# Scores and contexts of two graphs in one stretch of TensorE, in every second slot

## The chip, the cores and the metric

The kernel runs on one core of a Trainium2 chip. The metric is the device time of one launch in microseconds (us).

## The reference

Two layers of masked attention over 128 graphs of 128 nodes with 384 features, 6 heads of 64, each behind a layer norm with relu, with a residual sum. The adjacency matrix of a graph is the mask. Everything is float32.

```python
h = jnp.maximum(_layernorm(x, axis=-1), 0.0)
q = _heads(h @ Wq + bq)
k = _heads(h @ Wk + bk)
v = _heads(h @ Wv + bv)
scores = jnp.einsum('bhqd,bhkd->bhqk', q, k) / np.sqrt(HEAD_SIZE)
bias = jnp.where(graph_mask, 0.0, NEG)[:, None]
probs = jax.nn.softmax(scores + bias, axis=-1)
ctx = jnp.einsum('bhqk,bhkd->bhqd', probs, v)
x = x + (ctx.transpose(0, 2, 1, 3).reshape(...) @ Wf + bf)   # twice, with other weights
```

## The kernel before

**Units and slots.** Four graphs (`PER`) are a unit; there are 32 groups of graphs and 2 layers, so 64 units, numbered `t`. A unit takes four slots, `i` = 0 to 3. `over_slots` (L115) writes the slots out for every engine: units -1 to 5 unrolled, then a loop of 3 rounds over 14 units, then the rest unrolled. Each engine has its own `slot` function with a fixed order of operations, and works ahead or behind by a fixed number of slots; `graph_at(t, i, steps)` names the graph that lies `steps` behind or ahead. All waits are semaphores that count graphs (`unit_count`). Engines take their instructions strictly in this written order.

**A graph's way.** VectorE takes statistics of its rows (`statistics`), POOL the scale and shift (`norm`), ScalarE applies them with relu, VectorE transposes in blocks of 32 (`h_turn`), SP writes the blocks to HBM and reads them back so that the whole is transposed (`keep_blocks`, `bring_back`), and ScalarE and POOL split it into two fp16 parts, `ht_hi` and `ht_lo` (L616, L427). Products are made of three fp16 matmuls (`three`, L483): high times high, high times low, low times high. `project_v` makes v for one graph (9 matmuls of 384 columns), `project_qk` makes q and k for the whole unit, in 6 chunks of 3 pieces each; a piece is 3 matmuls of 512 columns, and `PIECES` (L54) spreads the 18 pieces over the four slots, 5, 4, 5, 4. `score` (L534) makes a graph's scores: 18 matmuls in tiles of 64 rows x 128 columns of the array, two at a time, one in each of two banks. VectorE adds the mask and takes the row maximum (`mask_and_max`, L829, six instructions), POOL negates it (`negate_max`), ScalarE takes the exp of six heads (`exp`), VectorE the reciprocal of the sums (`invert_sums`), POOL scales (`scale_probs`), VectorE turns blocks (`probs_turn`), and SP takes the probabilities through HBM. `apply_probs` (L517) makes a graph's context from float32 operands: 12 matmuls in tiles of 128 rows x 64 columns. ScalarE evicts the context as `ct_hi` (`ctx_hi`), VectorE the remainder as `ct_lo` (`ctx_lo`, which sets `ct_set`), `output` (L549) projects it (9 matmuls of 384 columns), and VectorE adds it to x in place (`add_residual`, which sets `out_added`).

**TensorE's order in a slot** (L567): v of the graph four ahead (`project_v(t + 1, i)`), scores of this graph, in odd slots contexts of the graphs 4 and 3 behind (`pair_at`, L111), pieces of qk, and the output of the graph 4 behind. ScalarE's order (L657): exp of the graph before, eviction of v, in odd slots two evictions of contexts, qk chunks, relu, `h_hi`, the mask in slot 2, qk chunks. VectorE's: `probs_turn` (2 behind), `h_turn` (9 ahead), `add_residual` (5 behind), `statistics` (11 ahead), `invert_sums` (1 behind), `mask_and_max` (this graph), in odd slots two `ctx_lo`, then `qk_lo_out`.

**Banks.** Of eight PSUM banks two hold scores (one graph), two contexts, one the output, one v, two the chunks of qk. The two banks of qk and v serve as output banks in the last two units.

Of the kernel before, what the change touches and what calls it, by code (L numbers as in the profile page):

```python
# [15 lines left out]
P = 128  # L16
# [5 lines left out]
def build(nc, x, adj, layers, out):  # L22
# [31 lines left out]
    PIECES = (((0, 1), (2, 3, 4)), ((5, 6), (7, 8)), ((9, 10), (11, 12, 13)), ((14, 15), (16, 17)))  # L54
# [56 lines left out]
    def pair_at(t, i):  # L111

        return [graph_at(t, i, -4), graph_at(t, i, -3)] if i % 2 else []
# [10 lines left out]
    with ExitStack() as ctx:  # L124
# [86 lines left out]
        largest_shared = sem("largest_shared")  # L211
        scales_set = sem("scales_set")
# [42 lines left out]
        def out_bank(t, i):  # L255

            return ps_out if t < LAST - 2 else (ps_v, ps_qk[0])[i % 2]
# [203 lines left out]
        def _(pe):  # L461
            def turn_largest(l):
                pe.wait_ge(largest_found, 5 * (l + 1))

                wait(pe, scales_set, l)
                pe.transpose(ps_out[0:6, 0:P], largest[:, :], ident[:, :]).then_inc(largest_turned, 1)

            def share_largest(l):
                pe.wait_ge(peaks_set, l + 1)
                pe.matmul(ps_out[:, 0:6], ones[0:6, :], peaks[:, :], start=True, stop=True).then_inc(largest_shared, 1)  # L470

            def sum_out_bias(l):
# [5 lines left out]
                acc = ps_ctx[0][:, 0:H]  # L478
# [9 lines left out]
            def project_v(t, i, m):  # L488
                b, l = unit_no(t) % 2, layer_of(t)
                pe.wait_ge(ht_set, unit_count(t, m, PER, i + 1))  # L490
                if unit_no(t) <= AHEAD and i == 0:
                    pe.wait_ge(weights_set, 4 * l + CAST_ORDER.index(2) + 1)

                wait(pe, v_set, unit_count(t, m, PER, i))
                rows = slice(i * NODES, (i + 1) * NODES)
                for c in range(KT):
                    mm = three(ps_v[:, 0:H], ht_hi[b][:, c, rows], ht_lo[b][:, c, rows], w_hi[l][2][:, c, :],
# [19 lines left out]
            def apply_probs(t, i, m):  # L517
                b = unit_no(t) % 2
                if (t, i) == (0, 0):
                    pe.wait_ge(out_bias_set, LAYERS)  # L520

                wait(pe, ct_set, unit_count(t, m, PER, i - 1))
                pe.wait_ge(v_set, unit_count(t, m, PER, i + 1))
                pe.wait_ge(p_back[i], unit_count(t, m, 16 * QUADS, 16 * QUADS))
                turned = p_moved[i % 2][:, :, :].rearrange("p a (s k) -> p s a k", s=HEADS)
                for c in range(PAIRS):
                    for odd in range(2):
                        hd = 2 * c + odd
                        mm = pe.matmul(ps_ctx[i % 2][odd * DH:(odd + 1) * DH, c * P:(c + 1) * P],  # L529
# [4 lines left out]
            def score(t, i, m):  # L534
# [3 lines left out]
                wait(pe, masked, unit_count(t, m, PER, i))  # L538
                cols = slice(i * NODES, (i + 1) * NODES)
                for c in range(PAIRS):  # L540
                    for q, k, first, last in ((qk_hi, qk_hi, True, False), (qk_hi, qk_lo, False, False),
                                              (qk_lo, qk_hi, False, True)):
                        for odd in range(2):
                            rows = slice(odd * DH, (odd + 1) * DH)
                            mm = pe.matmul(ps_scores[odd][:, c * P:(c + 1) * P], q[b][rows, c, cols],  # L545
# [3 lines left out]
            def output(t, i, m):  # L549
                l = layer_of(t)  # L550
                if t < LAST - 2:

                    wait(pe, out_added, unit_count(t, m, PER, i))
                else:

                    wait(pe, out_added, unit_count(t, m, PER, i - 1))
                if (t, i) == (0, 0):
                    pe.wait_ge(scales_set, LAYERS)
# [3 lines left out]
                for c in range(KT):  # L562
                    mm = three(out_bank(t, i)[:, 0:H], ct_hi[i % 2][:, c, :], ct_lo[i % 2][:, c, :], w_hi[l][3][:, c, :],
# [3 lines left out]
            def slot(t, m):  # L567
                for i in range(PER):
                    ou, oi = graph_at(t, i, -4)
                    if exists(t + 1):  # L570
                        project_v(t + 1, i, m)
                    if exists(t):
                        score(t, i, m)
                    for pu, pi in pair_at(t, i):
                        if exists(pu):
                            apply_probs(pu, pi, m)
                    if (t, i) == (0, 0):
# [8 lines left out]
                    if (t, i) == (0, 0):  # L586
# [9 lines left out]
        def _(act):  # L596
# [22 lines left out]
            def v_out(t, i, m):  # L619
# [5 lines left out]
                nc.scalar.activation(v[b][:, i, :], ps_v[:, 0:H], ACT.Copy).then_inc(v_set, 1)  # L625
# [299 lines left out]
```

## Time and profile before

| | |
|---|---|
| median of 3 runs | 1952.4 us (1952.3 to 1955.0) |
| the profiled execution | 1950.0 us, its span 1948.0 us |
| busy in the span: TensorE, ScalarE, VectorE, POOL | 1889.7, 1526.6, 1489.0, 1183.8 us |
| granted TensorE clock, mean | 0.992 of full speed |

The profile shows one execution. Busy time of an engine is time in which at least one of its compute instructions runs. Durations of matmuls overlap, as they are pipelined: the pace is the distance from start to start. The span begins and ends with stretches in which the pipeline fills and empties.

### The profile page before, as it was taken

Reading aid. Unit: us, or ns where it says so; the run is one execution under the profiler, and the core shown is the slowest. Engines: PE = TensorE matmul, PEld = TensorE weight load, DVE = VectorE, ACT = ScalarE, POOL = GpSimd, SP = SyncE. Lnnn points to the kernel's source line nnn. Section 1 sums busy time; section 2 is a strip of 40 time slices with the busy share of each in tenths; the row PEclk is TensorE's granted clock in tenths of the full one; section 3 lists DMA queues with packets and bytes.
Section 4 is the critical chain, followed back from the end, with each engine's and each line's share of the span. In section 5 each row is a group of like instructions: output and inputs, shape, how many; then the busy total and the mean of one; then the engine's idle time right before and its main releaser. Section 6 shows DMA issues by size and latency. Waiting matters only on the chain.

```text
span 1948.0 us, 58320 instructions
## 1 busy us (share of the span) xinstructions
PE 1889.7 (97%) x15766; PEld 1069.9 (55%) x15766; DVE 1489.0 (76%) x5312; ACT 1526.6 (78%) x4553; POOL 1183.8 (61%) x1800
## 2 busy tenths in 40 slices
PE   3899999999999999999999999999999999999996
PEld 1455555555555555555555555555555555555554
DVE  5687777777777777787777777787777777777765
ACT  3688888888888787887887788887887887887874
POOL 3576666666666566666665566666666666666642
PEclk9999999999999999999999999999999999999998
DMA  6466656666666566666665665666666666655554
GB/s 184 134 184 182 197 180 197 192 197 195 199 191 184 175 200 200 201 183 194 188 197 181 194 191 182 199 199 194 196 190 185 195 198 203 189 180 176 178 165 155
DMA packets 445248, 365.36 MB, mean 188 GB/s; under 512 B 212450, under 2 KB 412132, under 8 KB 444900
## 3 DMA queue, kind: packets, MB, share of 16 engines
q1 hardware_dynamic: 444900, 361.43, 60.4%
q8 instruction: 132, 2.16, 0.5%
q14 instruction: 216, 1.77, 0.3%
HBM read 185.09 MB, written 176.16 MB: 185 GB/s over the span
## 4 chain that ended last, share of the span: by engine, by line
PE 91%; SPq 3%; DMA 2%; issue 1%; DVE 1%; ACT 1%; POOL 0%; POOLq 0%; DVEq 0%; ACTq 0%
PE ps_qk L484 14%; PE ps_qk L485 12%; PE ps_qk L486 12%; PE ps_ctx L529 9%; PE ps_scores L545 8%; PE ps_v L484 6%; PE ps_v L485 6%; PE ps_v L486 6%; PE ps_out L484 6%; PE ps_out L486 6%; PE ps_out L485 6%; SPq L322 2%; DMA h_dram<-h_blocks 1%; ACT probs L646 1%; DMA wf_raw<-in_L_gnn_Wf 0%
## 5 line engine op out<-in xcount | busy, mean ns | idle before, releaser
L646 ACT ACTIVATE probs<-probs,exp_bias,exp_scale 128x128 f32<-128x128 f32 x1536 | 735.7, 482 | 35.2 <-POOL exp_bias L415 26.9
L420 POOL TENSOR_TENSOR probs<-probs,row_rcp 128x768 f32<-128x768 f32 x256 | 376.2, 1469 | 272.9 <-DVE row_rcp L806 272.9
L816 DVE SCALAR_TENSOR_TENSOR qk_lo<-ps_qk,qk_bias,qk_hi 128x512 f16<-128x512 f32 x384 | 288.0, 751 | 250.7 <-ACT qk_hi L630 249.6
L829 DVE CUSTOM_DVE_ANT_0 probs<-ps_scores,mask 128x128 f32<-128x128 f32 x1536 | 345.7, 287 | 97.2 <-PE ps_scores L545 69.7
L427 POOL TENSOR_TENSOR ht_lo<-h_moved,ht_hi 128x384 f16<-128x384 f32 x256 | 234.6, 916 | 287.8 <-ACT ht_hi L616 287.8
L630 ACT ACTIVATE qk_hi<-ps_qk,qk_bias 128x512 f16<-128x512 f32 x384 | 263.7, 687 | 101.0 <-PE ps_qk L486 83.8
L625 ACT ACTIVATE v<-ps_v 128x384 f32<-128x384 f32 x256 | 122.9, 480 | 223.4 <-PE ps_ctx L529 222.2
L646 ACT ACTIVATION_READ_ACCUMULATOR probs<-probs,exp_bias,exp_scale 128x1 f32 x1536 | 289.8, 189 | 0.0
L409 POOL TENSOR_TENSOR x_tile<-x_tile,out_bias 128x384 f32<-128x384 f32 x256 | 256.0, 1000 | 0.0
L484 PE MATMUL ps_v<-wv_hi,ht_hi 128*128 128x384 f16 x768 | 250.7, 326 | 4.4 <-issue 2.5
L782 DVE STREAM_TRANSPOSE p_blocks<-probs 128x768 f32<-128x768 f32 x256 | 248.1, 969 | 7.6 <-issue 5.6
L485 PE MATMUL ps_v<-wv_lo,ht_hi 128*128 128x384 f16 x768 | 250.6, 326 | 0.0
L486 PE MATMUL ps_v<-wv_hi,ht_lo 128*128 128x384 f16 x768 | 250.5, 326 | 0.0
L484 PE MATMUL ps_out<-wf_hi,ct_hi 128*128 128x384 f16 x744 | 242.5, 326 | 0.0
L485 PE MATMUL ps_out<-wf_lo,ct_hi 128*128 128x384 f16 x744 | 242.5, 326 | 0.0
L486 PE MATMUL ps_out<-wf_hi,ct_lo 128*128 128x384 f16 x744 | 242.5, 326 | 0.0
L484 PE MATMUL ps_qk<-ht_hi,wq_hi 128*128 128x512 f16 x576 | 221.2, 384 | 11.6 <-POOL ht_lo L427 6.9
L484 PE MATMUL ps_qk<-ht_hi,wk_hi 128*128 128x512 f16 x576 | 220.8, 383 | 3.4 <-DVE qk_lo L816 3.4
L485 PE MATMUL ps_qk<-ht_lo,wq_hi 128*128 128x512 f16 x576 | 220.1, 382 | 0.0
L486 PE MATMUL ps_qk<-ht_hi,wq_lo 128*128 128x512 f16 x576 | 219.8, 382 | 0.0
L485 PE MATMUL ps_qk<-ht_lo,wk_hi 128*128 128x512 f16 x576 | 219.7, 381 | 0.0
L486 PE MATMUL ps_qk<-ht_hi,wk_lo 128*128 128x512 f16 x576 | 219.6, 381 | 0.0
(99 smaller groups left out, 3484.9 us busy)
## 6 DMA issues: line engine op xcount, KB each, us to landing
p_dram<-p_blocks SPq DMA_DIRECT2D x256, 384.0 KB, 2.4
p_moved<-p_dram SPq DMA_DIRECT2D x1024, 96.0 KB, 2.4
h_dram<-h_blocks SPq DMA_DIRECT2D x256, 192.0 KB, 2.3
h_moved<-h_dram SPq DMA_DIRECT2D x1024, 48.0 KB, 1.9
x_tile<-in_x SPq DMA_DIRECT2D x128, 192.0 KB, 2.8
out_x<-x_tile SPq DMA_DIRECT2D x128, 192.0 KB, 2.5
adj_u<-in_adj SPq DMA_DIRECT2D x64, 64.0 KB, 2.4
wv_raw<-in_L_gnn_Wv SPq DMA_DIRECT2D x2, 576.0 KB, 5.0
```

Source lines behind the costliest of these rows:

```text
L409: nc.gpsimd.tensor_tensor(xs, xs, out_bias[l][:, :], ALU.add).then_inc(res_ready, 1)
L420: nc.gpsimd.tensor_tensor(probs[i % 2][:, :, :], probs[i % 2][:, :, :], row_rcp[i % 2][:, :].rearrange("p (a o) -> p a o", o=1) .to_broadc ...
L427: nc.gpsimd.tensor_tensor(in_order(ht_lo[b][:, :, rows]), moved_in_order(h_moved[i % 2]), in_order(ht_hi[b][:, :, rows]), ALU.subtract).th ...
L484: pe.matmul(acc, a_hi, b_hi, start=first, stop=False)
L485: pe.matmul(acc, a_hi, b_lo, start=False, stop=False)
L486: return pe.matmul(acc, a_lo, b_hi, start=False, stop=last)
L529: mm = pe.matmul(ps_ctx[i % 2][odd * DH:(odd + 1) * DH, c * P:(c + 1) * P], v[b][:, i, hd * DH:(hd + 1) * DH], turned[:, odd * PAIRS + c, ...
L630: nc.scalar.activation(qk_hi[b][:, chunk, :], ps_qk[chunk % QK_BANKS][:, :], ACT.Identity, bias=qk_bias[layer_of(t)][:, chunk // KT, chunk ...
L646: ins = nc.scalar.activation(probs[i % 2][:, s, :], probs[i % 2][:, s, :], ACT.Exp, bias=exp_bias[i % 2][:, s:s + 1], scale=exp_scale[laye ...
L782: return nc.vector.transpose(out.rearrange("p b (c k) -> p b c k", c=cols), view.rearrange("p (c b r) -> p b c r", c=cols, b=QUADS))
L816: nc.vector.scalar_tensor_tensor(out=qk_lo[b][:, chunk, :], in0=ps_qk[chunk % QK_BANKS][:, :], scalar=qk_bias[layer_of(t)][:, chunk // KT, ...
L829: ins = nc.vector.tensor_tensor_reduce(probs[i % 2][:, s, :], ps_scores[s // PAIRS][:, (s % PAIRS) * P:(s % PAIRS + 1) * P], mask[b][:, i, ...
```

## The change

TensorE's order becomes different in even and odd slots. In an even slot it makes the scores of this graph and of the next, then the contexts of the graphs 4 and 3 behind, then pieces of qk, then v, then the output of the graph 4 behind. In an odd slot it makes only pieces of qk, v and an output. `PIECES` becomes 4, 5, 4, 5. In unit -1 v stays ahead of qk. Four banks hold the scores of two graphs. Two banks are left for contexts, outputs and v: context and output of a graph use bank `i % 2`, its v bank `1 - i % 2`. So v of an even slot follows the second context in its bank (it waits for `ct_set`), v of an odd slot follows the output before it (it waits for `out_added`), the first context follows v of the slot before (`v_set`), the second context the output of the slot before (`out_added`), and the output of an odd graph follows a v (`v_set`). On ScalarE the eviction of v moves from behind exp to the slot's end, and the context evictions into even slots; on VectorE `add_residual` moves ahead of `h_turn`, and `ctx_lo` into even slots. The set-up of layer 1 (largest values, output bias) moves into the last slot of unit -1 and uses two of the score banks; a semaphore `largest_taken` is added for it.

```diff
-    PIECES = (((0, 1), (2, 3, 4)), ((5, 6), (7, 8)), ((9, 10), (11, 12, 13)), ((14, 15), (16, 17)))
+    PIECES = (((0, 1), (2, 3)), ((4, 5), (6, 7, 8)), ((9, 10), (11, 12)), ((13, 14), (15, 16, 17)))
...
-        return [graph_at(t, i, -4), graph_at(t, i, -3)] if i % 2 else []
+        return [] if i % 2 else [graph_at(t, i, -4), graph_at(t, i, -3)]
...
-        ps_scores = [bank("ps_scores0"), bank("ps_scores1")]
-        ps_ctx = [bank("ps_ctx0"), bank("ps_ctx1")]
-        ps_out = bank("ps_out")
-        ps_v = bank("ps_v")
+        ps_scores = [bank(f"ps_scores{k}") for k in range(4)]
+        ps_shared = [bank("ps_shared0"), bank("ps_shared1")]
...
+        def score_bank(i, odd):
+            return ps_scores[2 * (i % 2) + odd]
+
+        def ctx_bank(i):
+            return ps_shared[i % 2]
+
+        def out_bank(i):
+            return ps_shared[i % 2]
+
+        def v_bank(i):
+            return ps_shared[1 - i % 2]
...
@@ project_v @@
-                wait(pe, v_set, unit_count(t, m, PER, i))
+                cu, ci = graph_at(t, i, -7)
+                ou, oi = graph_at(t, i, -9)
+                if i % 2 == 0 and exists(cu):
+
+                    pe.wait_ge(ct_set, unit_count(cu, m, PER, ci + 1))
+                elif i % 2 and exists(ou):
+
+                    pe.wait_ge(out_added, unit_count(ou, m, PER, oi + 1))
+                else:
+
+                    wait(pe, v_set, unit_count(t, m, PER, i - 1))
...
@@ apply_probs @@
-                wait(pe, ct_set, unit_count(t, m, PER, i - 1))
-                pe.wait_ge(v_set, unit_count(t, m, PER, i + 1))
+                vu, vi = graph_at(t, i, 5 if i % 2 else 7)
+                if (i % 2 == 0 or (t, i) == (0, 1)) and exists(vu):
+
+                    pe.wait_ge(v_set, unit_count(vu, m, PER, vi + 1))
+                else:
+
+                    pe.wait_ge(out_added, unit_count(t, m, PER, i - 1))
+                    pe.wait_ge(v_set, unit_count(t, m, PER, i + 1))
...
@@ score @@
-                wait(pe, masked, unit_count(t, m, PER, i))
+                wait(pe, masked, unit_count(t, m, PER, i - 1))
...
@@ output @@
+                vu, vi = graph_at(t, i, 7)
+                if i % 2 and exists(vu):
+
+                    pe.wait_ge(v_set, unit_count(vu, m, PER, vi + 1))
...
@@ slot of TensorE @@
-                    if exists(t + 1):
-                        project_v(t + 1, i, m)
-                    if exists(t):
+                    if exists(t) and i % 2 == 0:
                         score(t, i, m)
+                        score(t, i + 1, m)
                     for pu, pi in pair_at(t, i):
                         if exists(pu):
                             apply_probs(pu, pi, m)
-                    if (t, i) == (0, 0):
-                        sum_out_bias(1)
+                    if t == FIRST:
+                        project_v(t + 1, i, m)
                     if exists(t + 1):
                         for piece in PIECES[i][0] + PIECES[i][1]:
                             project_qk(t + 1, piece, m)
+                    if exists(t + 1) and t != FIRST:
+                        project_v(t + 1, i, m)
                     if exists(ou):
                         output(ou, oi, m)
                     if (t, i) == (-1, 3):
                         turn_largest(1)
-                    if (t, i) == (0, 0):
+                        sum_out_bias(1)
                         share_largest(1)
...
@@ slot of ScalarE @@
-                    if exists(t + 1):
-                        v_out(t + 1, i, m)
...
                         for chunk in chunks_done(i, 1):
                             qk_hi_out(t + 1, chunk, m)
+                        v_out(t + 1, i, m)
...
@@ slot of VectorE @@
+                    if exists(ou):
+                        add_residual(ou, oi, m)
                     if exists(hu):
                         h_turn(hu, hi, m)
-                    if exists(ou):
-                        add_residual(ou, oi, m)
```

## Rows read from the trace of the kernel before

**Rows 1.** Page, part 4: shares of the chain that ended last, by engine.
```profile
PE 91%; SPq 3%; DMA 2%; issue 1%; DVE 1%; ACT 1%; POOL 0%; POOLq 0%; DVEq 0%; ACTq 0%
```

**Rows 2.** TensorE's waits, 100 to 1900 us: total, times, longest.
```profile
PE ps_ctx L529 <- DMA p_moved<-p_dram: 4.0, 2, 2.1
PE ps_v L484 <- issue: 2.5, 2, 1.3
```

**Rows 3.** Busy time by stretch: length, then each engine's busy time (instructions).
```profile
50.00:100.00 50.00, 44.67 (x287) 21.91 (x285) 34.25 (x127) 33.42 (x90) 29.48 (x46) 0.93 0.47 135
...
1850.00:1948.00 98.00, 82.47 (x716) 47.42 (x714) 58.30 (x220) 58.28 (x193) 34.41 (x40) 0.95 0.49 159
```

**Rows 4.** Chain that ended last, in order of time: start, length, what.
```profile
1086.21 1.46 PE ps_ctx L529 x24
...
1901.95 1.46 PE ps_ctx L529 x24
```

**Rows 5.** Timeline of TensorE, one odd and one even slot: start, us, instruction.
```profile
1007.07 0.33 PE L486 MATMUL ps_v<-wv_hi,ht_lo 128*128 128x384 f16 x1
...
1007.33 0.23 PE L545 MATMUL ps_scores<-qk_hi 64*128 64x128 f16 x2
...
1007.78 0.22 PE L545 MATMUL ps_scores<-qk_hi,qk_lo 64*128 64x128 f16 x2
...
1007.93 1.53 PE L529 MATMUL ps_ctx<-p_moved,v 128*64 128x128 f32 x24
...
1009.40 0.39 PE L484 MATMUL ps_qk<-ht_hi,wq_hi 128*128 128x512 f16 x1
...
1012.00 0.33 PE L484 MATMUL ps_out<-wf_hi,ct_hi 128*128 128x384 f16 x1
...
1013.46 0.33 PE L484 MATMUL ps_v<-wv_hi,ht_hi 128*128 128x384 f16 x1
...
1014.76 0.33 PE L486 MATMUL ps_v<-wv_hi,ht_lo 128*128 128x384 f16 x1
...
1015.02 0.23 PE L545 MATMUL ps_scores<-qk_hi 64*128 64x128 f16 x2
...
1015.63 0.39 PE L484 MATMUL ps_qk<-ht_hi,wk_hi 128*128 128x512 f16 x1
```

**Rows 6.** Timeline of VectorE around slot 0 of a unit.
```profile
1024.33 1.02 DVE L810 TENSOR_TENSOR ct_lo<-ps_ctx,ct_hi 128x384 f16<-128x384 f32 x2 [0.25 <-ACT ct_hi L638]
...
1028.15 0.97 DVE L782 STREAM_TRANSPOSE p_blocks<-probs 128x768 f32<-128x768 f32 x1
...
1029.04 0.54 DVE L782 STREAM_TRANSPOSE h_blocks<-h 128x384 f32<-128x384 f32 x1
...
1029.50 0.58 DVE L839 SCALAR_TENSOR_TENSOR x_tile<-ps_out,out_scale,x_tile 128x384 f32<-128x384 f32 x1
...
1030.85 0.19 DVE L806 RECIPROCAL row_rcp<-row_sum 128x6 f32<-128x6 f32 x1
...
1031.42 0.29 DVE L829 CUSTOM_DVE_ANT_0 probs<-ps_scores,mask 128x128 f32<-128x128 f32 x1 [0.38 <-issue]
...
1033.07 0.75 DVE L816 SCALAR_TENSOR_TENSOR qk_lo<-ps_qk,qk_bias,qk_hi 128x512 f16<-128x512 f32 x1 [0.29 <-ACT qk_hi L630]
```

**Rows 7.** Timeline of ScalarE: first exp of a graph, and what follows the sixth.
```profile
1027.35 0.48 ACT L646 ACTIVATE probs<-probs,exp_bias,exp_scale 128x128 f32<-128x128 f32 x1
...
1030.21 0.47 ACT L625 ACTIVATE v<-ps_v 128x384 f32<-128x384 f32 x1
```

**Rows 8.** Chain, near the end: between VectorE's `ct_lo` and TensorE's `ps_out`.
```profile
1943.10 0.14 issue
```

**Rows 9.** Page, part 6, and a row of SP's timeline.
```profile
p_dram<-p_blocks SPq DMA_DIRECT2D x256, 384.0 KB, 2.4
p_moved<-p_dram SPq DMA_DIRECT2D x1024, 96.0 KB, 2.4
...
1031.98 2.72 SPq L322 DMA_DIRECT2D p_moved<-p_dram  x4
```

More of the change, by code:

```diff
@@ L253, in x_of @@
             return x_tile[group_of(t) % X_BUFFERS]
-        def out_bank(t, i):
-            return ps_out if t < LAST - 2 else (ps_v, ps_qk[0])[i % 2]
+        def score_bank(i, odd):
[6 more added lines that the diff above has]
+            return ps_shared[1 - i % 2]
+        ps_largest, ps_bias = ps_scores[2], ps_scores[3]
         def moved_in_order(tile):
@@ L463, in turn_largest @@
                 pe.wait_ge(largest_found, 5 * (l + 1))
-                wait(pe, scales_set, l)
-                pe.transpose(ps_out[0:6, 0:P], largest[:, :], ident[:, :]).then_inc(largest_turned, 1)
+                wait(pe, largest_taken, l)
+                pe.transpose(ps_largest[0:6, 0:P], largest[:, :], ident[:, :]).then_inc(largest_turned, 1)
             def share_largest(l):
                 pe.wait_ge(peaks_set, l + 1)
-                pe.matmul(ps_out[:, 0:6], ones[0:6, :], peaks[:, :], start=True, stop=True).then_inc(largest_shared, 1)
+                pe.matmul(ps_largest[:, 0:6], ones[0:6, :], peaks[:, :], start=True, stop=True).then_inc(largest_shared, 1)
             def sum_out_bias(l):
@@ L477, in sum_out_bias @@
                 wait(pe, out_bias_set, l)
-                acc = ps_ctx[0][:, 0:H]
+                acc = ps_bias[:, 0:H]
                 for c in range(KT):
@@ L492, in project_v @@
                     pe.wait_ge(weights_set, 4 * l + CAST_ORDER.index(2) + 1)
-                wait(pe, v_set, unit_count(t, m, PER, i))
+                cu, ci = graph_at(t, i, -7)
[6 more added lines that the diff above has]
+                    wait(pe, v_set, unit_count(t, m, PER, i - 1))
                 rows = slice(i * NODES, (i + 1) * NODES)
                 for c in range(KT):
-                    mm = three(ps_v[:, 0:H], ht_hi[b][:, c, rows], ht_lo[b][:, c, rows], w_hi[l][2][:, c, :],
+                    mm = three(v_bank(i)[:, 0:H], ht_hi[b][:, c, rows], ht_lo[b][:, c, rows], w_hi[l][2][:, c, :],
                                w_lo[l][2][:, c, :], c == 0, c == KT - 1)
@@ L528, in apply_probs @@
                         hd = 2 * c + odd
-                        mm = pe.matmul(ps_ctx[i % 2][odd * DH:(odd + 1) * DH, c * P:(c + 1) * P],
+                        mm = pe.matmul(ctx_bank(i)[odd * DH:(odd + 1) * DH, c * P:(c + 1) * P],
                                        v[b][:, i, hd * DH:(hd + 1) * DH], turned[:, odd * PAIRS + c, :, :],
@@ L544, in score @@
                             rows = slice(odd * DH, (odd + 1) * DH)
-                            mm = pe.matmul(ps_scores[odd][:, c * P:(c + 1) * P], q[b][rows, c, cols],
+                            mm = pe.matmul(score_bank(i, odd)[:, c * P:(c + 1) * P], q[b][rows, c, cols],
                                            k[b][rows, KT + c, cols], start=first, stop=last)
@@ L562, in output @@
                 for c in range(KT):
-                    mm = three(out_bank(t, i)[:, 0:H], ct_hi[i % 2][:, c, :], ct_lo[i % 2][:, c, :], w_hi[l][3][:, c, :],
+                    mm = three(out_bank(i)[:, 0:H], ct_hi[i % 2][:, c, :], ct_lo[i % 2][:, c, :], w_hi[l][3][:, c, :],
                                w_lo[l][3][:, c, :], c == 0, c == KT - 1)
@@ L624, in v_out @@
                 act.wait_ge(v_projected, unit_count(t, m, PER, i + 1))
-                nc.scalar.activation(v[b][:, i, :], ps_v[:, 0:H], ACT.Copy).then_inc(v_set, 1)
+                nc.scalar.activation(v[b][:, i, :], v_bank(i)[:, 0:H], ACT.Copy).then_inc(v_set, 1)
             def qk_hi_out(t, chunk, m):
@@ L809, in ctx_lo @@
                 dve.wait_ge(ct_hi_set, unit_count(t, m, PER, i + 1))
-                nc.vector.tensor_tensor(ct_lo[i % 2][:, :, :], ps_ctx[i % 2][:, 0:H].rearrange("p (c k) -> p c k", c=KT),
+                nc.vector.tensor_tensor(ct_lo[i % 2][:, :, :], ctx_bank(i)[:, 0:H].rearrange("p (c k) -> p c k", c=KT),
                                         ct_hi[i % 2][:, :, :], ALU.subtract).then_inc(ct_set, 1)
@@ L894, in _ @@
             find_peaks(0)
+            take_largest(0)
             find_scales(0)
```

35 lines of the change are left out of this document (17 added, 18 removed).

## The prediction

> **What bounds the kernel now.** I read the chain of work that ended last first: nine tenths of the span run through TensorE, the rest is start and end [rows 1]. The waits of TensorE between 100 and 1900 us say how solid that is: 6.5 us in two rows, all at the two jumps back of the loop (a wait for probabilities coming back, and an instruction stream that was not there yet) [rows 2]. So in that stretch the time is TensorE's own stream, and only what shortens this stream, or puts a wait into it, counts. Outside it TensorE is busy 44.67 of 50 us in the second half of the start and 82.47 of the last 98 [rows 3].
>
> The stream repeats. Every second slot has a stretch of 24 context matmuls, and its place in the chain moves from 1086.21 to 1901.95 us in 56 steps: 14.567 us for a pair of slots [rows 4]. In the timeline of one odd and one even slot [rows 5] the reader is to look at the distances between starts, not at durations, since matmuls overlap. Nine matmuls of `ps_out` take 13.46 - 12.00 = 1.46 us, 0.163 each, and `ps_v` has the same shape. Nine pairs of scores start 0.45/8 = 0.056 apart. Twelve matmuls of `ps_qk` take 2.60, 0.216 each. Where the shape of the tile changes, the next start comes later than this rhythm: v to scores 1007.33 - 1007.07 - 0.16 = 0.10; scores to context 0.15 - 0.06 = 0.09; scores to qk 15.63 - 15.02 - 9 x 0.056 = 0.10; v to scores of the even slot 0.10 again. The 24 context matmuls with the change behind them take 1.47; a row of 24 that lasts 1.53, the last of which lasts about 0.22 to 0.28 past its start, gives a rhythm near 0.055, and so some 0.15 for context to qk. A pair thus has five changes, 0.54 us of 14.57.
>
> By the Trainium skill ("TensorEngine Tiling (Array Packing)", Key Properties) a change of the tiling mode drains the array, and by "TensorE: Matmul & The Clock Gate" (Single matmul latency) a matmul that can't hide its fill and drain costs 398 cycles at 2.4 GHz over its columns, 0.166 us; an estimate from that page for two changes a pair would be 0.33 us, 41 us in all, and 1911. The starts close the period without such a remainder, so the rows decide, and the page's figure is not used.
>
> **The change, part by part.** Per pair of slots the matmuls stay the same in number and shape. The order becomes: even slot scores, scores, context, context, 4 pieces of qk, v, output; odd slot 5 pieces of qk, v, output.
>
> 1. *Changes of shape.* Before: v-scores, scores-context, context-qk, v-scores, scores-qk. After: output-scores, scores-context, context-qk. Two go, 0.10 + 0.10 = 0.20 us a pair [rows 5]. From about 100 to 1907 us there are 123 pairs (1807 less 6.5 of waits, by 14.57): 24.5 us. The new change (output-scores) is between the same two shapes as v-scores. Bounds for the two: 0.18 to 0.22, 22 to 27 us.
>
> 2. *The shared banks: the wait that can bind.* Let T be the start of an even slot on TensorE. Scores begin at 0.10, context at 0.10 + 2 x 0.51 + 0.09 = 1.20, qk at 2.67, v at 5.26, output at 6.72, and the odd slot at 8.19; there v begins at 3.24 and the slot ends at 6.17. Sum 14.36, which is 14.57 less 0.20. Now v of the even slot goes into the bank that held the second context, so it waits for `ct_set`, VectorE's `ct_lo`. In VectorE's order that stands behind residual, `h_turn`, statistics, reciprocal and the six masks. The residual waits for the last output matmul, which ends at T + 0.17. VectorE's rows [rows 6]: residual to reciprocal 1.35, `h_turn` 0.46 (0.54 where the next operation doesn't overlap it), reciprocal to first mask 0.57 in slot 0 (of which 0.38 is issue, for three semaphores counted in a register; in slot 2 it is two, so some 0.2 less), masks 33.07 - 0.29 - 31.42 = 1.36, the two `ct_lo` 1.02. A semaphore from VectorE to TensorE takes 0.14 [rows 8]; I take it both ways. Sum: 0.31 + 0.46 + 1.35 + 0.57 + 1.36 + 1.02 + 0.14 = 5.21, against 5.26. That is no cover worth the name: with `h_turn` at 0.54 it is 5.29. In slot 2 the sum is about 5.0 to 5.1. So I charge 0 to 0.1 us in one slot of four, 0 to 6 us in 62 units, and take 2.
>
> 3. *What feeds that chain.* ScalarE's eviction of v stands at the end of the slot, and exp of the graph before waits behind it. In the odd slot v ends at 3.24 + 1.30 + 0.33 = 4.87; eviction (0.47) and six exp (2.86 with its reads, [rows 7]) end at about 8.3, which is T + 2.1 to 2.2 of the next slot; the reciprocal would start at 0.31 + 0.46 + 1.35 = 2.12. Again level. In the even slot the same: v ends 6.89, exp ends 10.3, 2.1 after the odd slot's start. In the odd slot VectorE has to be back for the residual at 6.17 + 0.31 = 6.48: 2.12 + 0.37 + 1.36 + two `qk_lo` of at most 0.75 + turn of probabilities 0.89 [rows 6] ends near 6.2, so 0.2 to 0.3 is left. POOL's order is unchanged and it is the least busy of the four.
>
> 4. *The other new waits.* First context of an even slot waits for `v_set` of the odd slot before: set at 5.4 of 6.17, wanted at T + 1.20. Second context waits for the residual: ready at 0.31 + 0.58 + 0.14 = 1.03, wanted at 1.93. v of the odd slot waits for the residual of the last output: ready at 1.03, wanted at 3.24. Output of the odd slot waits for the eviction of v: 2.7 us earlier. The second scores wait for the masks of the graph before, which end near 3.9 in the odd slot. Each costs nothing, and if its cover went by 1 us it still would. Behind each of them stands the whole rest of TensorE's queue, so a miss counts in full.
>
> 5. *Probabilities back.* The odd graph is now wanted one slot earlier, at T + 1.93 of an even slot. Its turn ends about 0.9 us before an odd slot begins; writing to HBM 2.4, then four reads that SP issues in 1.7 to 2.7 us (the longest seen with two loads ahead of them, [rows 9]) and 2.4 to land: at the latest 7.9, wanted at 6.17 + 1.93 = 8.1. SP is also held by `h_turn` before these reads. Usual slack over 1 us, worst 0.2; the adjacency load stands only in even slots, beside reads that have 7 us to spare. Cost 0, bounds 0 to 2 us.
>
> 6. *Jumps of the loop.* They cost 3.3 us each now [rows 2]. With less slack on VectorE the stall of its own stream comes through, while the wait for probabilities shrinks: -2 to +4 us for both, taken 0.
>
> 7. *Start and end.* The output bias of layer 1 (3 us of TensorE) moves ahead of the first scores, the context of graph 0 moves from slot 3 to slot 4, and the casts of layer-1 weights in unit 1 lengthen VectorE's and ScalarE's slots by over 1 us each where no slack is left. Bounds from what TensorE idles in the start row, 5.3 us [rows 3]: -2 to +5, taken +2. At the end the scores no longer stand behind outputs that wait for probabilities, but the last output follows the one before: of the 15.5 us idle there -3 to +2, taken -1.
>
> Sum, against the profiled execution (1950.0 us, span 1948.0): 1950.0 - 24.5 + 2 + 0 + 2 - 1 = 1928.5. The median of the runs shown is 2.4 above that execution (1952.4), and a new median may lie like it: I forecast 1930.
>
> **The rivals.** (a) *VectorE's chain takes a good part of the gain.* Items 2 and 3 are sums of ten terms with no slack in one slot and 0.2 in the other. If the chain is 0.2 to 0.3 longer in practice (contention, a later exp), v waits 0.25 in slot 0 and 0.1 in slot 2, 0.35 a unit, 62 x 0.35 = 22 us off the gain: 1950. For it: the level sums. Against: all terms are distances of starts from rows, overlaps and issue included. At 0.1 to 0.2 longer it gives 1936 to 1945. (b) *Slower: exp closes a loop.* TensorE's v, its eviction, exp, reciprocal, masks, `ct_lo` and the next v form a ring through three engines. If exp ends 0.5 late in every slot, v waits 0.45 in slot 0 and 0.3 in slot 2, 0.38 a pair: 123 x (0.38 - 0.20) = 22 us slower, 1974. It decides from a wait of 0.20 us a pair on. Against it: ScalarE's rows run without gaps and leave 0.1 at most. (c) *The gaps are not saved*: they come back between the two graphs' scores or as an issue gap behind the waits; 1952. Against: 24 context matmuls of two graphs already run with two waits inside and no gap [rows 5]. (d) *More than forecast*: the jumps and the start get shorter, 1950 - 27 - 4 - 2 and no stall: 1917 to 1921.
>
> **How the numbers follow.** Forecast 1922 to 1936: 0.66. Rival (a), mild, 1936 to 1945: 0.12, and up to 1952: 0.05. (b): 0.06. (c): 0.05. (d): 0.06. What a measurement here can tell from no change is about 0.2%, 3.9 us. Faster is forecast, mild (a) and (d), and a sliver of the rest: 0.85; same 0.08; slower 0.07. The range that leaves 2 in 10 out goes from 1919 to 1943.
>
> **What would show it.** A pair of slots at 14.36 us; one stretch of 36 scores, 24 contexts; no idle of TensorE before `ps_v` beyond 0.1 us and none before `ps_ctx`; VectorE's `ct_lo` ending close ahead of the first v matmul. A row "PE ps_v waits for DVE ct_lo" with tens of us would be (a) or (b), and exp's end against the reciprocal's start tells which. A pair at 14.57 without waits would be (c). The prediction is wrong if one of items 4 or 5 has a row of its own.

## The result, and the profile after

The changed kernel takes 1939.9 us (median of 12 runs, 1935.6 to 1950.8) against 1953.8 (1948.9 to 1958.8) for the kernel before: a ratio of 0.9927, 95% interval 0.9913 to 0.9940. The forecast was 1930, its range 1919 to 1943. The profiled execution takes 1940.7 us, its span 1938.7, at a granted clock of 0.995 (before 0.992). Against the profiled execution before, 9.3 us are gained where the sum had 21.5.

The chain that ended last, by engine and by line (page of the kernel after, part 4; compare [rows 1]):

```profile
PE 50%; SPq 28%; DMA 9%; issue 8%; ACT 2%; DVE 2%; POOL 1%; POOLq 0%; DVEq 0%; ACTq 0%
SPq L332 21%; PE ps_qk L494 7%; DMA p_dram<-p_blocks 7%; PE ps_shared L494 7%; PE ps_shared L496 7%; PE ps_shared L495 7%; PE ps_qk L496 7%; PE ps_qk L495 7%; PE ps_shared L551 5%; PE ps_scores L571 4%; SPq L324 2%; ACT probs L669 1%; SPq L104 1%; SPq L293 1%; SPq L340 1%
```

TensorE carried 91% of it before, now 50%. SP's queue (L332 issues the reads that bring blocks back) and the transfers, most of them of probabilities, hold 37%. TensorE's waits from 100 to 1900 us (total, times, longest; compare [rows 2]):

```profile
PE ps_shared L551 <- DMA p_moved<-p_dram: 8.7, 19, 1.0
PE ps_scores L571 <- issue: 3.9, 2, 2.3
PE ps_shared L494 <- DVE ct_lo L835: 1.1, 3, 0.8
PE ps_shared L551 <- DVE x_tile L864: 0.5, 1, 0.5
```

The first row is the news: 19 times contexts wait for probabilities, where before they did so only at the two jumps of the loop. All 19 lie between 250 and 1430 us, in the loop. The pairs of slots, read from the chain as in [rows 4]:

```profile
152.06 1.46 PE ps_shared L551 x24
166.42 1.46 PE ps_shared L551 x24
180.78 1.46 PE ps_shared L551 x24
...
1885.10 1.46 PE ps_shared L551 x24
```

Undisturbed pairs are 14.36 us apart, as summed. The 119 pairs from 152.06 to 1885.10 take 1733.0 = 119 x 14.356 + 24.7. In the same view of the kernel before the row to compare with is

```profile
144.94 1.46 PE ps_ctx L529 x24
```

and from it to 1901.95 [rows 4] there are 120 pairs: 1757.0 = 120 x 14.567 + 9.0. So the changes of shape gave 0.21 a pair, some 25 us, and 15.7 us of new idle time in scattered pairs took more than half of it back.

### The profile page after: what moved, and what is told of

It is laid out like the page before. It is cut to its first block, busy times and chain, and to the rows that moved or that the text cites. A ratio compares the mean times of both kernels' runs of the same rounds, so it can differ in the third digit from the quotient of the medians.

```text
span 1938.7 us, 58154 instructions
## 1 busy us (share of the span) xinstructions
PE 1869.9 (96%) x15766; PEld 1079.6 (56%) x15766; DVE 1479.7 (76%) x5312; ACT 1526.5 (79%) x4553; POOL 1185.7 (61%) x1800
## 4 chain that ended last, share of the span: by engine, by line
PE 50%; SPq 28%; DMA 9%; issue 8%; ACT 2%; DVE 2%; POOL 1%; POOLq 0%; DVEq 0%; ACTq 0%
SPq L332 21%; PE ps_qk L494 7%; DMA p_dram<-p_blocks 7%; PE ps_shared L494 7%; PE ps_shared L496 7%; PE ps_shared L495 7%; PE ps_qk L496 7%; PE ps_qk L495 7%; PE ps_shared L551 5%; PE ps_scores L571 4%; SPq L324 2%; ACT probs L669 1%; SPq L104 1%; SPq L293 1%; SPq L340 1%
## 5 line engine op out<-in xcount | busy, mean ns | idle before, releaser
L841 DVE SCALAR_TENSOR_TENSOR qk_lo<-ps_qk,qk_bias,qk_hi 128x512 f16<-128x512 f32 x384 | 279.7, 747 | 112.7 <-ACT qk_hi L653 111.5
L648 ACT ACTIVATE v<-ps_shared 128x384 f32<-128x384 f32 x256 | 125.6, 491 | 259.4 <-PE ps_shared L496 259.3
L864 DVE SCALAR_TENSOR_TENSOR x_tile<-ps_shared,out_scale,x_tile 128x384 f32<-128x384 f32 x256 | 157.6, 616 | 195.5 <-PE ps_shared L496 195.3
L494 PE MATMUL ps_shared<-wf_hi,ct_hi 128*128 128x384 f16 x768 | 251.7, 328 | 3.8 <-DVE ct_lo L835 3.8
L494 PE MATMUL ps_shared<-wv_hi,ht_hi 128*128 128x384 f16 x768 | 250.9, 327 | 1.9 <-DVE ct_lo L835 1.1
L495 PE MATMUL ps_shared<-wf_lo,ct_hi 128*128 128x384 f16 x768 | 251.6, 328 | 0.0
L496 PE MATMUL ps_shared<-wf_hi,ct_lo 128*128 128x384 f16 x768 | 251.6, 328 | 0.0
L496 PE MATMUL ps_shared<-wv_hi,ht_lo 128*128 128x384 f16 x768 | 250.9, 327 | 0.0
L495 PE MATMUL ps_shared<-wv_lo,ht_hi 128*128 128x384 f16 x768 | 250.9, 327 | 0.0
L551 PE MATMUL ps_shared<-p_moved,v 128*64 128x128 f32 x3072 | 204.5, 279 | 18.1 <-DMA p_moved<-p_dram 17.2
```

What stands on the lines that cost most here:

```text
L494: pe.matmul(acc, a_hi, b_hi, start=first, stop=False)
L495: pe.matmul(acc, a_hi, b_lo, start=False, stop=False)
L496: return pe.matmul(acc, a_lo, b_hi, start=False, stop=last)
L551: mm = pe.matmul(ctx_bank(i)[odd * DH:(odd + 1) * DH, c * P:(c + 1) * P], v[b][:, i, hd * DH:(hd + 1) * DH], turned[:, odd * PAIRS + c, :, :],
L841: nc.vector.scalar_tensor_tensor(out=qk_lo[b][:, chunk, :], in0=ps_qk[chunk % QK_BANKS][:, :], scalar=qk_bias[layer_of(t)][:, chunk // KT, ...
```

## Where the new wait comes from

Timeline of the kernel after. First VectorE's turn of one odd graph's probabilities, then what SP issues from then on (start, us, instruction), then the two halves of the contexts on TensorE:

```profile
699.51 0.97 DVE L807 STREAM_TRANSPOSE p_blocks<-probs 128x768 f32<-128x768 f32 x1
```
```profile
697.95 3.48 SPq L332 DMA_DIRECT2D p_moved<-p_dram  x4
701.72 1.73 SPq L332 DMA_DIRECT2D h_moved<-h_dram  x4
703.78 0.34 SPq L324 DMA_DIRECT2D p_dram<-p_blocks  x1
704.50 0.34 SPq L324 DMA_DIRECT2D h_dram<-h_blocks  x1
705.05 0.34 SPq L340 DMA_DIRECT2D out_x<-x_tile  x1
705.70 0.34 SPq L293 DMA_DIRECT2D x_tile<-in_x  x1
706.32 1.75 SPq L332 DMA_DIRECT2D p_moved<-p_dram  x4
```
```profile
708.76 0.88 PE L551 MATMUL ps_shared<-p_moved,v 128*64 128x128 f32 x12
710.28 0.88 PE L551 MATMUL ps_shared<-p_moved,v 128*64 128x128 f32 x12 [0.64 <-DMA p_moved<-p_dram]
```

The turn ends at 700.48, but its write is issued at 703.78: SP is still in its own round, with four reads that took 3.48 us instead of the usual 1.75. The write lands 2.4 later, and the reads go out from 706.32 on. The last of them is issued at 707.63 and lands 2.5 later, at 710.14. The second half should start 0.66 after the first (12 matmuls at 0.055) and starts 1.52 after it, so 0.86 is lost where the row says 0.64: idle time is counted only past the drawn-out end of the matmul before. That is why the rows give 8.7 us and the starts of the stretches 17.2, in 35 pairs, 3.2 of them at the loop's jumps.

I call the time from the end of a turn to the issue of its write the lag. From 250 to 1430 us (the loop) its median in the kernel before is 0.09 us for even graphs, whose probabilities are wanted first, and 2.26 for odd ones, which have time. After, it is 1.79 and 2.19, and now the odd graph is wanted in the slot where it was not before. In the loop the contexts are late by over 0.1 us in 29 pairs of 81. There the lag of the odd graph is 2.7 us in the mean, in the others 1.9; its own four reads take the usual 1.8 in both, and the last of them lands about 0.3 later than in the others. From 1470 to 1850 us (no loop) the lag is 0.83 and 0.43, and there TensorE doesn't wait.

SP's own waits in the loop alone say why it is behind. Kernel before, then after (250 to 1430 us, 161 rounds of SP, one a slot):

```profile
SPq L105 <- DMA p_dram<-p_blocks: 69.5, 68, 1.6
SPq L105 <- DVE p_blocks L782: 15.5, 35, 1.1
SPq L105 <- PE ps_ctx L529: 3.9, 10, 0.6
```
```profile
SPq L106 <- DMA p_dram<-p_blocks: 73.7, 70, 2.9
SPq L106 <- DVE h_blocks L807: 4.4, 10, 1.0
```

After the change SP waits for another engine only 10 times in 161 rounds; else it issues, or it waits for its own write to land. A round takes 7.33 us in the mean, and 7.30 without the waits for engines; a slot of TensorE that nothing disturbs takes 7.18. Before, these were 7.21 and 7.28. (The 7.33 alone says nothing: with one round a slot, SP's mean round is TensorE's mean slot, whoever is the slower. The waits for engines tell them apart.) Behind the loop, from 1470 to 1850 us, a round without the waits for engines takes 6.1. One reason stands in SP's timeline there:

```profile
1506.97 1.83 SPq L332 DMA_DIRECT2D p_moved<-p_dram  x4
1508.90 1.80 SPq L332 DMA_DIRECT2D h_moved<-h_dram  x4
1510.80 0.38 SPq L324 DMA_DIRECT2D p_dram<-p_blocks  x1
```

Between the end of one group and the start of the next lie 0.10 us here and about 0.28 in the loop (701.43 to 701.72 above), where each wait's count is first put into a register. Without any of its waits a round takes 6.8 us in the mean in the loop and 5.6 behind it; some six such gaps a round, about 1.1 us by this estimate, are most of the difference. So the register-counted waits are a part of the round's length; no run took them out.

Over the whole span another row is SP's longest, and it misleads:

```profile
SPq L97 <- DVE h_blocks L807: 77.8, 65, 5.0
```

In the kernel before it was

```profile
SPq L96 <- DVE h_blocks L782: 10.9, 4, 5.0
```

since `h_turn` stood right behind `probs_turn`, and the change put the residual in between. But L97 is the wait of the unrolled units, where TensorE loses next to nothing. In the loop the wait for `h_blocks` is on L106, the 4.4 us above.

## The experiments

The theory: SP runs behind in its own queue, and this makes the odd graph's probabilities late. Rivals: VectorE's chain through `ct_lo` (a), the exp ring (b), or only the loop's register-counted waits. All edits are to the changed kernel unless said; ratios are to the kernel before.

**Pieces ahead.** Two of an even slot's four pieces of `project_qk` go ahead of the scores, so the contexts come later against SP.

```diff
+                    ahead = 2 if i % 2 == 0 and t != FIRST else 0
+                    if exists(t + 1):
+                        for piece in pieces[:ahead]:
+                            project_qk(t + 1, piece, m)
                     if exists(t) and i % 2 == 0:
                         score(t, i, m)
...
-                        for piece in PIECES[i][0] + PIECES[i][1]:
+                        for piece in pieces[ahead:]:
```

> The changed kernel with one edit: in even slots two of the four qk pieces stand ahead of the scores, so the contexts come 1.3 us later in the slot and everything else keeps its place. Number and kind of shape changes stay three a pair. Theory A (the loss against the sum is the second context waiting for probabilities that SP brings back about 2 us later than assumed, against a point of need 1.1 us earlier): the rows of TensorE waiting for p_moved nearly vanish (8.7 us between 100 and 1900 us now), pairs in the loop go from 14.36 to 15.6 back to 14.36, and the time falls by 10 to 15 us against the changed kernel, ratio to before 0.985 to 0.988. Rival B (SP's queue as such is the bound in the loop, whatever the point of need): at most 3 us less, ratio 0.991 to 0.993. Rival C (VectorE's chain into v is the bound): no gain, and more waits of ps_shared for ct_lo, since the second context is evicted 1.3 us later; ratio 0.993 or above.

Measured: 0.9961 (0.9945 to 0.9976), not faster than the changed kernel, if anything slower. The waits for probabilities fell to 3.4 us, 7 times. But v now starts earlier behind the contexts: six matmuls of qk stand between instead of twelve, and from their first to v there are 1.40 us instead of 1.30 in every pair (the pair is 14.45), with 5.2 more in places. The deadline was moved and the gain paid out to `ct_lo`: the two waits pull at the same stretch of TensorE from both sides.

**Turn first.** VectorE does `h_turn` ahead of `add_residual` again, as before.

```diff
-                    if exists(ou):
-                        add_residual(ou, oi, m)
                     if exists(hu):
                         h_turn(hu, hi, m)
+                    if exists(ou):
+                        add_residual(ou, oi, m)
```

> The changed kernel with VectorE's old order in a slot: h_turn ahead of the residual. Theory A with this cause (SP stands at the write of h_blocks until h_turn, which now waits behind the residual and so behind TensorE's last output, and this puts SP behind): SP's wait for h_turn falls from 77.8 us to some 10, the distance from the end of the turn of probabilities to its write falls from a median of 1.8 to 2.2 us to under 1 for the odd graphs, waits for p_moved fall by more than half; 6 to 12 us less than the changed kernel, ratio 0.987 to 0.990. Rival B (SP's queue is full of its own issues): no change, 0.992 to 0.994. Rival C: less wait for ct_lo, at most 3 us.

Measured: 0.9929 (0.9904 to 0.9954). The expected gain is not there. SP's wait for `h_blocks` went back to 10.5 us, the lag in the loop to 1.14 and 1.62 (1.51 and 1.94 in a second execution of the unedited kernel, below), the waits for probabilities to 5.3 us, 7 times. The profiled execution is 9.6 us shorter (1931.1), the fastest of its five, yet the ratios can't tell the two kernels apart. The long row shrank to a seventh and the time hardly moved; what the edit is worth in the loop is not resolved.

**Loads on ScalarE.** The loads of x and of the adjacency matrix are issued by ScalarE at the start of its slot, and no longer by SP.

```diff
@@ slot of ScalarE; the same lines leave SP's slot @@
+                    if i == 0 and exists(t + 2):
+                        load_adj(t + 2, m)
+                    if exists(t + 4) and layer_of(t + 4) == 0:
+                        load_x(t + 4, i, m)
                     if exists(pu):
                         exp(pu, pi, m)
```

> The changed kernel with the loads of x and of the adjacency matrix issued by ScalarE at the start of its slot instead of by SP. Theory A: SP gets 0.65 us free in every slot of half the units and catches up sooner; 2 to 6 us less, ratio 0.989 to 0.992. Rival B (SP's queue is the bound by its own issues): 10 us less or more, ratio 0.988 or below. Rival C: no gain, or a loss of up to 0.3 us a slot where ScalarE's exp ends later, ratio 0.993 to 0.996.

Measured: 1.0139 (1.0105 to 1.0172). ScalarE's and TensorE's waits:

```profile
ACT probs L686 <- issue: 62.4, 112, 6.6
```
```profile
PE ps_shared L490 <- DVE ct_lo L856: 37.7, 46, 4.4
```

No context waits for probabilities. In the changed kernel the first row is 6.6 us, 2 times, at the loop's jumps. This is rival (b) made by hand: exp starts late by the issue, and reciprocal, masks, `ct_lo` and v of the next slot follow. The time from the first of twelve qk matmuls to v rises from 2.60 to 2.755 in the median pair, with 38.2 more in places.

**Scores apart.** The odd graph's scores go back to the start of the odd slot; contexts and banks stay.

```diff
-                    if exists(t) and i % 2 == 0:
+                    if exists(t):
                         score(t, i, m)
-                        score(t, i + 1, m)
```

> The changed kernel with the scores of the odd graph moved back to the start of the odd slot; banks, waits, contexts and all other engines stay. It puts back the two shape changes that the change had removed (output to scores and scores to qk in the odd slot). By the sum of the prediction a pair takes 14.36 + 0.20 = 14.56 us where nothing waits, 123 x 0.20 = 24.5 us; as this also gives SP 0.20 us more a pair, part of the waits for p_moved goes, so 12 to 24 us more than the changed kernel in all, ratio 0.999 to 1.005. Rival (what was gained did not come from the shape changes): a pair of 14.36 and a ratio near 0.993.

Measured: 1.0184 (1.0152 to 1.0216), slower than the kernel before and beyond the expected 1.005. TensorE's waits:

```profile
PE ps_shared L494 <- DVE ct_lo L834: 18.2, 48, 0.8
```

Output to scores takes 1.56 twice a pair, so two of the changes of shape are back (0.20 a pair), and without the 0.5 of the second scores as cover v of every even slot in the loop starts later than 2.60 after the first qk matmul: 2.88 in slot 2 and 3.08 in slot 0 (medians). Behind the loop it stays at 2.60. So v starts 5.04 after slot 2 begins and 5.24 after slot 0 begins: the chain that item 2 put at 5.0 to 5.1 and 5.21.

**The changed kernel again, with one piece ahead, and with loads in a gap.** All ran on one chip. The second has Turn first and one piece ahead; the third issues the loads from ScalarE just before it evicts v in even slots, where it waits for TensorE.

> The changed kernel itself, unedited, so that the kernels of this group can be compared with it on one chip. Ratio to before 0.991 to 0.994 as in the result; between 5 and 30 pairs of slots lengthened by waits for p_moved.

> The changed kernel with h_turn ahead of the residual on VectorE and one qk piece (not two) ahead of the scores in even slots. With two pieces ahead the waits for p_moved shrank from 19 to 7, but v then waited about 0.10 us in every pair for ct_lo, since the second context was evicted 1.3 us later. If that is how the gain was given back, 0.65 us later is still inside VectorE's cover: a pair of 14.36 us without a standing wait before v, and waits for p_moved in fewer than 8 pairs; 8 to 14 us less than the changed kernel, ratio to it 0.993 to 0.996. If instead the pieces ahead cost by themselves (another order of shapes), the pair stays at 14.44.

> The changed kernel with the loads of x and adjacency issued by ScalarE, but only in even slots and just before the eviction of v, where ScalarE stands idle about 1 us waiting for TensorE. This takes the same load off SP as the loads at the start of ScalarE's slot did, without standing ahead of exp. If the loss of that run came from exp being late in the ring exp, reciprocal, masks, ct_lo, v, its wait for ct_lo (37.7 us) is gone here, and what is left is the effect of SP's load alone: waits for p_moved fall by more than half, 6 to 12 us less than the changed kernel, ratio to it 0.994 to 0.997. If ScalarE's issuing costs more than its gap, v is evicted late and waits for ct_lo come back.

Measured: 0.9916 (0.9903 to 0.9930); 0.9914 (0.9901 to 0.9928); 0.9983 (0.9974 to 0.9992). The lags of the first are 1.51 and 1.94 with 9.4 us of waits, of the second 1.85 and 1.98 with 5.7. In the first SP's round in the loop, without its waits for engines, is 7.21 us: in both executions it is level with the slot of 7.18 or above it. So one piece ahead with Turn first gains nothing over the changed kernel, against an expected 0.4 to 0.7%. The third is the lesson: up to two DMAs a slot fewer on SP, and yet lags of 2.06 and 2.33 and 14.0 us of waits, 27 times. SP's row for the landing of its write, in the loop, went from 73.7 us, 70 times, to

```profile
SPq L106 <- DMA p_dram<-p_blocks: 177.0, 160, 3.4
```

SP issued those loads in the time in which it waits for the landing in any case; taking them away frees nothing. That this kernel is even 0.7% slower than the changed one is not explained.

**All three together**, loads in the gap, one piece and Turn first.

> All three: h_turn first, one piece ahead, loads in ScalarE's gap. No standing wait left between the start and the end except at the loop's jumps (about 8 us): 1806 - 16 = 1790 us from slot 4 to slot 252, 14 to 18 us less than the changed kernel, ratio to it 0.991 to 0.993, about 1925 us; near the prediction made for the change itself.

Measured: 0.9957 (0.9943 to 0.9970), slower than the changed kernel and not faster, with 7.7 us of waits for probabilities and 4.7 for `ct_lo`.

**SP fills its wait.** SP's round becomes: write probabilities, read h of the slot before, write h, store and loads, read probabilities. The reads of h thus lie where SP waits for the landing.

```diff
                     if exists(pu):
                         keep_blocks(pu, pi, p_blocked, p_blocks, p_dram, p_kept, p_back, m)
+                    lu, li = graph_at(t, i, 8)
+                    if t >= 1 and (t, i) != (1, 0) and exists(lu):
+                        bring_back(lu, li, h_dram, h_moved, h_kept, h_back, ht_set, m)
...
-                    if exists(hu):
+                    if exists(hu) and t < 1:
                         bring_back(hu, hi, h_dram, h_moved, h_kept, h_back, ht_set, m)
```

> The changed kernel with another order on SP from unit 1 on: write of p_blocks, reads of the h of the slot before, write of h_blocks, loads and stores, reads of p. So the 2.35 us that the queue stands until the write of p_blocks has landed are filled with h's four reads (1.75 us); before, only the loads stood there. The last group showed that taking the loads off SP frees nothing: they lay in that wait. Theory A2: SP's cycle in the loop is 6.5 us, with one stall of 1.1 us every two slots, 14.1 of the 14.36 us of a pair, so it can't make up what it has lost and probabilities come late; with the wait filled the cycle is near 5 us, the distance from the turn's end to its write falls to about 0.1 us for both graphs, the waits for p_moved outside the loop's jumps go, and 10 to 16 us go with them: ratio to before 0.984 to 0.988. Rival D (the probabilities are late because HBM transfers themselves are slower in these stretches, not because SP issues them late): no change in the waits, ratio 0.991 to 0.993. A loss is possible where h now arrives late for ScalarE's ht_hi, which would show as a wait of ht_hi for h_moved.

Measured: 1.0102 (1.0086 to 1.0119). The lag is gone (0.08 and 0.09), and it is slower. Waits of ScalarE (whole span) and of TensorE (100 to 1900 us):

```profile
ACT ht_hi L642 <- DMA h_moved<-h_dram: 156.3, 171, 8.1
```
```profile
PE ps_shared L554 <- DMA p_moved<-p_dram: 23.1, 34, 1.8
```

h has landed 10.5 us after its turn (median in the loop) instead of 8.9, and ScalarE takes it up 10.0 after it in the changed kernel; so now ScalarE waits for it, 171 times in 256 graphs. Everything behind it moves, and the turn of probabilities ends 0.3 to 0.6 us later in its slot. A lag of zero behind a late turn helps nobody. The same SP order in the kernel *before* and together with Turn first:

> The same order of SP's queue in the kernel before. There the probabilities of the graph that is wanted first leave SP 0.09 us after their turn already, and TensorE waits for them only at the loop's two jumps. Theory A2: nothing to gain but at the jumps, 0 to 4 us, ratio 0.998 to 1.000. If the new order is better by itself in some other way, the gain is as large here as in the changed kernel.

> SP's new order and h_turn ahead of the residual on VectorE, in the changed kernel. Theory A2: the lag on SP is gone with the new order alone, so this adds at most 2 us; ratio to before 0.983 to 0.988. If h_turn behind the residual was a cause of its own for the lag, it adds 4 us or more.

Measured: 1.0490 (1.0463 to 1.0517), with 314.1 us of ScalarE's waits for h; and 1.0121 (1.0103 to 1.0138). All three forecasts missed. This order is bad in both kernels, and the test says nothing for or against the theory, since it moved a second wait.

**Half of h's reads.** What was missing was a test that shortens SP's round and moves nothing. Two of the four reads of h are left out, so this kernel lacks part of its data.

```diff
-                for quad in range(QUADS):
+                for quad in range(2 if back is h_back and t > 0 else QUADS):
                     sp.dma_start(moved[i % 2][quad * SQ:(quad + 1) * SQ, :, :],
...
-                act.wait_ge(h_back[i], unit_count(t, m, 16 * QUADS, 16 * QUADS))
+                act.wait_ge(h_back[i], unit_count(t, m, 32, 64))
```

The waits that count these reads count two of four; that of SP ahead of its write, changed likewise, is not shown.

> The changed kernel with two of the four reads of h per graph left out from unit 1 on (the other half of h keeps old values, so this kernel leaves out part of the data of q, k and v; every arithmetic instruction stays). SP then issues six reads a slot instead of eight, about 0.87 us less (four take 1.75), nothing is moved to another engine, and h is back earlier rather than later. Theory A (the probabilities of the odd graph are late because SP's own round of issues is too long, and that is where the missing part of the gain went): SP's lag behind VectorE's turn of probabilities falls from 1.8 and 2.2 us to under 1 in the loop, TensorE's waits for the probabilities from 8.7 us (9.4 in the second execution) to under 2, and the time by 8 to 17 us against the changed kernel: 1919 to 1932 for a kernel before at 1950, a ratio of 0.984 to 0.990. Theory B (SP's lag is only where the waits show, and something else paces the ring, exp or VectorE): the lag falls, but the time stays within 4 us of the changed kernel, ratio 0.990 to 0.994, with new waits for ct_lo or a late exp. Theory C (the loss comes with the register-counted waits of the loop): lag and waits stay as they are.

Measured: 0.9859 (0.9840 to 0.9877), 1921.3 us beside 1948.7, clear of both measurements of the changed kernel (0.9927 and 0.9916). Lag 0.12 and 0.08. The chain is TensorE's again, and its 119 pairs from the first to the last row shown take 1717.4 = 119 x 14.356 + 9.1, and 9.0 is what the kernel before loses:

```profile
PE 91%; DVE 2%; ACT 2%; DMA 2%; issue 2%; SPq 1%; POOL 0%; POOLq 0%; DVEq 0%; ACTq 0%
```
```profile
147.47 1.46 PE ps_shared L554 x24
...
1864.91 1.46 PE ps_shared L554 x24
```

TensorE's waits, 100 to 1900 us, and SP's in the loop, 250 to 1430 us:

```profile
PE ps_shared L497 <- DVE ct_lo L838: 5.2, 7, 1.9
PE ps_scores L574 <- issue: 2.3, 2, 1.2
PE ps_shared L554 <- DMA p_moved<-p_dram: 1.6, 2, 1.4
```
```profile
SPq L106 <- DVE h_blocks L810: 171.2, 155, 2.1
SPq L106 <- DVE p_blocks L810: 105.3, 114, 1.8
SPq L106 <- DMA p_dram<-p_blocks: 13.3, 36, 1.3
SPq L106 <- PE ps_shared L554: 4.6, 19, 0.2
```

Now SP stands ready and waits for VectorE in nearly every round. Without the waits for engines its round is 5.5 us instead of 7.30. That is more than the 0.87 of two issues: the reads of h took 2.14 us in the mean in the changed kernel, since 59 of 161 groups were over 2.2, and take 0.82 here; the rest is mostly time no longer spent on the write's landing.

The kernel also moves fewer bytes; but the median landing times of the probabilities hardly differ (2.4 us for the write in both, 2.4 instead of 2.5 for a read), while the lag fell by 1.7 and 2.1. And h is back earlier, but ScalarE takes it up at the same time as before (9.9 us after its turn, was 10.0) and waited for it only 3.2 us in the changed kernel. The whole new loss of 15.7 us is gone with this edit, which settles the place of the loss: the length of SP's round. Register-counted waits alone would have left the lag as it was (theory C); as a part of the round they stay possible. How much of the loss is due to the issues, to the counts in registers and to the slow groups, the test can't tell.

## Why the prediction was right and where it was off

*Right.* Item 1: the pair is 14.356, as summed; measured starts are 1.11 us from 36 scores to contexts, 1.46 contexts to qk, 1.56 output to scores. By the estimate from the Trainium skill ("TensorE: Matmul & The Clock Gate", Single matmul latency; "TensorEngine Tiling (Array Packing)", Key Properties) two changes would be 0.33 us; the trace has 0.21, so the measurement decides against it. Items 2 and 3: the chain through VectorE just holds, as summed, and the starts of v in Scores apart (5.04 and 5.24) meet the sums. By the starts v came 2.0 us late in all outside the jumps (1.1 in the waits' row), charged 2; rival (a) did not happen, and (b) only when the loads were put on ScalarE. Item 4: 0.5 us in all. Item 6: by the starts the jumps cost 9.0 us before (6.5 in the rows) and 8.8 after, taken 0. Item 7: start +0.45 instead of +2, end 0 instead of -1.

*Off: item 5*, taken 0 with bounds 0 to 2, where 13 to 14 us stayed (15.7 less the 2.0 of item 2). Each of its durations holds: write 2.4, reads 1.75 to 3.48, landing 2.4. What it put at nothing, without a reason, is the lag: it began at the end of the turn on VectorE, as if SP stood ready there, and in the kernel before SP did so for even graphs only. Nor does its total follow from its terms: from 0.9 before the odd slot, 2.4, then 1.7 to 2.7, then 2.4 give 5.6 to 6.6, not 7.9, so by its own terms the slack against 8.1 was 1.5 at worst and 2.5 as a rule. Take from the usual slack the median lag of 2.2, and 0.3 is left, which is used up in the pairs with a lag near 3. The lag of the odd graph could be read before predicting: 2.26 in the trace of before, harmless there. The prediction named its own sign of being wrong, a row of its own for item 5, and the row is there: 8.7 us. Item 5 also said that SP is "held by `h_turn`" and put no number to it; that wait is real (77.8 us instead of 10.9), but it lies outside the loop and cost next to nothing. With what was measured the sum closes: 1950.0 less 25.1 (119 x 0.211), plus 15.7 for items 2 to 6 together, plus 0.45 of the start, is 1941.0 against 1940.7. The forecast missed by 10 us of 1930. That the result was inside the range is partly luck: its upper end was there for rival (a), a different mechanism of the same size.

*Open.* Why SP sometimes takes 2.2 to 3.5 us for four reads that else take 1.75 is not explained: 74 of 322 groups between 250 and 1430 us, and 81 of 321 in the kernel before. That the loss lies in the loop fits SP's longer round there (7.30 against 6.1), but no run took the counts out of the registers. No version beat the changed kernel clearly that computes everything; a way to bring h back with fewer issues would be the one to look for.

## What to carry to other kernels

When a change brings a deadline forward, measure in the trace of before how far the queue that serves it runs behind its producer, for the very item that becomes urgent; an in-order queue whose round, without its waits for engines, is as long as the period (7.30 us against 7.18 here) has no slack, however short each transfer is. Count those waits in the stretch where the time is lost: the longest row of the whole span, 77.8 us, stood elsewhere. Which instruction of a queue may be taken away for a gain is decided by where it waits: two loads in the shadow of a landing gave nothing, two reads outside it gave back the whole 15.7 us. And a cure for one queue must be followed to what it delays: filling the shadow with h's reads gave ScalarE 156 us of waits.

## What the runs showed of the hardware

Each of the two changes of shape that went away (fp16 matmuls in 128x128 tiles followed by fp16 matmuls in 64x128 tiles, and back) cost about 0.10 us on TensorE, 0.21 us for both, hardly varying over 120 pairs. A DMA issued by ScalarE holds up its arithmetic: 116 loads of x and 63 of the adjacency matrix gave 62.4 us of idle time ahead of exp, 112 times, where the changed kernel has 6.6 us, 2 times. On SP the issue of a write takes 0.34 us, of four reads 1.75, and in 74 of 322 groups 2.2 to 3.5, without a row that names a reason. Between two groups SP needs 0.10 us where its counts are constants and 0.28 where they stand in registers.
